# Gathering eight edges per index in the target stages of a three-layer graph network, with the layers' float32 split moved to ScalarE and TensorE

## The reference

```python
msg = h[src][:, None, :] * attn[src][:, :, None]
neigh = jax.ops.segment_sum(msg, dst, num_segments=n)
out = elu(neigh.reshape(n, -1) @ weight)
x = layernorm(x + out)
...
def layer(nf, traj, src, dst, We, be, Wn, bn):
    ef = concatenate([nf[src], nf[dst], traj[:, None]], -1)
    msg = leaky_relu(ef @ We.T + be, 0.01)
    red = segment_sum(msg, dst, nf.shape[0])
    return leaky_relu(concatenate([nf, red], -1) @ Wn.T + bn, 0.01)
# three layers, then layernorm(x + h)
```

## Time and profile before

| | us |
|---|---|
| median of 3 runs | 12386.24 (12385.78 to 12394.3) |
| span of the profiled execution | 10659.1 |
| grouping of the edges, attention scores | 2318 |
| source stage 0 / its target stage | 757 / 1382 |
| source stages 1, 2, 3 | 581, 579, 580 |
| target stages 1, 2, 3 | 1347, 1322, 1347 |

### The profile page before, as it was taken

One profiled execution on the slowest core, in us unless ns is written; L12 is line 12 of the kernel. 1 busy time (PEld: TensorE's weight loads), 2 busy tenths in 40 slices (PEclk: granted clock), 3 DMA queues, 4 the chain that ended last, 5 costly groups with the idle time before them and its releaser, 6 DMA issues. The chain is left out here.

```text
span 10659.1 us, 520405 instructions
## 1 busy us (share of the span) xinstructions
PE 8373.3 (79%) x180770; PEld 7503.4 (70%) x180770; DVE 9593.9 (90%) x19091; ACT 5558.6 (52%) x17135; POOL 5206.2 (49%) x5854
## 2 busy tenths in 40 slices
PE   7999999669976666589867776997777699766775
PEld 6999999347755555478766765886667678766774
DVE  6999999579989999778899996889999878899997
ACT  7888886027768888567422223673222267422222
POOL 0000000671027777534577773447777634577773
PEclk9999999569988888679988888998888799988887
DMA  1000000136556666758766675886766858766665
GB/s 43 9 8 8 8 8 7 38 93 216 216 185 195 195 195 195 132 184 294 247 193 200 204 204 89 291 294 210 205 205 205 167 173 295 255 194 202 205 204 89
DMA packets 1255800, 1748.08 MB, mean 164 GB/s; under 512 B 219360, under 2 KB 866418, under 8 KB 1254770
## 3 DMA queue, kind: packets, MB, share of 16 engines
q1 hardware_dynamic: 1009055, 1185.35, 34.1%
q0 software_dynamic: 245760, 549.71, 21.4%
q10 hardware_dynamic: 304, 4.93, 0.1%
HBM read 1049.39 MB, written 694.49 MB: 164 GB/s over the span
## 5 line engine op out<-in xcount | busy, mean ns | idle before, releaser
L1823 POOL DMA_INDIRECT work<-rows,quad_at x2928 | 2953.2, 1009 | 1028.6 <-issue 900.7
L1664 PE MATMUL bank<-work 128*128 128x64 bf16 x46848 | 2185.8, 209 | 997.8 <-DVE work L1911 997.5
L1664 PEld LDWEIGHTS bank<-work 128*128 128x128 fp8e4 (+1 forms) x46848 | 1979.2, 109 | 1062.6 <-issue 1033.2
L1848 ACT COPY work<-tabs 128x192 bf16 x2928 | 1029.4, 352 | 2942.2 <-PE bank L1864 2670.1
L1864 PE MATMUL bank<-work 128*128 128x64 bf16 x35136 | 1527.0, 208 | 274.2 <-DMA work<-hits_g 242.5
L1864 PEld LDWEIGHTS bank<-work 128*128 128x128 fp8e4 x35136 | 1382.8, 108 | 307.9 <-issue 235.6
L1608 PE MATMUL bank<-work 128*128 128x64 bf16 x34560 | 1565.2, 193 | 3.7 <-issue 3.7
L1608 PEld LDWEIGHTS bank<-work 128*128 128x128 fp8e4 x34560 | 1410.1, 98 | 175.3 <-issue 8.2
L1627 DVE TENSOR_SCALAR work<-bank,part 128x512 fp8e4<-128x512 f32 x1440 | 1026.8, 750 | 284.1 <-PE bank L1588 283.5
L1898 DVE TENSOR_TENSOR work<-bank,work 128x512 f32<-128x512 f32 x1464 | 1061.2, 739 | 238.3 <-PE bank L1864 138.2
L1695 POOL DMA_INDIRECT work<-rows,quad_at x976 | 990.1, 1014 | 416.3 <-PE bank L1664 216.8
(11 more groups left out here) (361 smaller groups left out, 18753.2 us busy)
## 6 DMA issues: line engine op xcount, KB each, us to landing
work<-hits_g SPq DMA_DIRECT2D x1464, 256.0 KB
rows<-work SPq DMA_DIRECT2D x1440, 256.0 KB, 3.3
hits_g<-work SPq DMA_DIRECT2D x976, 128.0 KB
rows<-work SPq DMA_DIRECT2D x480, 260.0 KB
work<-hits_s SPq DMA_DIRECT2D x720, 128.0 KB, 3.2
work<-rows,quad_at POOLq DMA_INDIRECT x3904
hits_s<-work SPq DMA_DIRECT2D x240, 128.0 KB
side<-meta POOLq DMA_DIRECT2D x720, 20.0 KB, 3.2
```

Source lines behind the costliest of these rows:

```text
L1664: last = ten.matmul(to[:, 0:D], hits_of(j), piece_of(j), start=j == 0 and k == 0, stop=j == QUAD - 1 and k == 2, skip_group_check=True)
L1823: pool.indirect_dma_start(quads[g // 2 % (GATHERED // 2)][:, half(g)], None, table, bass.IndirectOffsetOnAxis(ap=quad_at[:, g:g + 1], axis ...
L1848: sca.copy(window[q % 4].unsqueeze(1), tabs[:, 1, bass.ds(w, 1), :]).then_inc(s_window, 1)
```

## The change

An index names eight slots (an oct, two quads that lie together: 2 KB, 2,080 bytes in stage 0). So that the two quads lie together, the source stages store each group by itself: a partition writes two pieces of 1 KB. The number of groups of a target stage is 584 in place of 976, each with twice the slots; a group's stored matrices are 256 KB. The real groups (counted from `src` and `dst` of the reference by the kernel's numbering of slots) were 893 of the 976 and are 510 of the 584; the other 83 and 74 are the filling.

Stage 0 keeps its steps with operands twice as wide. In the layers everything goes by single groups: DVE adds (512 columns, PSUM and gathered rows, into `total`), and writes the leaky ReLU back to the PSUM bank of the group. ScalarE casts the bank to bf16 (`high`); TensorE subtracts that in the bank by a matmul with minus the identity (`minus_b`, 512 columns); ScalarE casts the rest (`mid`), TensorE subtracts again, ScalarE casts `low`. The scatter takes the three. POOL gathers four groups ahead of the add.

```diff
-NG = 976
+OCT = 8
+NG = 584
...
-        to_rows = table.rearrange("(l p g) c -> l p (g c)", p=P, g=GROUP_LOT)
+        to_rows = table.rearrange("(l g p) c -> l g p c", p=P, g=GROUP_LOT)
...
-                syn.dma_start(to_rows[bass.ds(l, 1), :, :].rearrange("l p c -> (l p) c"), made[n]).then_inc(s_out[n], 16)
+                syn.dma_start(to_rows[bass.ds(l, 1), :, :, :].rearrange("l g p c -> p (l g) c"),
+                              made[n].rearrange("p (g c) -> p g c", g=GROUP_LOT)).then_inc(s_out[n], 16)
...
-        HITS, AROUND, LAG, BATCH = 8, 16, 5, 4
+        AROUND, HITS, ROWS, WINDOWS, BANKS, MIDS, LOWS = 24, 8, 4, 4, 6, 6, 4
+        LESS, LESSER, SCATTER, KEEP = 2, 3, 5, 6
...
+                at_least(pool, s_added, g - ROWS + 1, since)
+                pool.indirect_dma_start(octs[g % ROWS], None, table_octs,
+                                        bass.IndirectOffsetOnAxis(ap=oct_at[:, g:g + 1], axis=0)).then_inc(s_octs[g % GATHERED], 16)
...
+                window_of(g, q)
+                if begun(g, LESSER + 3):
+                    low_of(g - LESSER - 3, (q - LESSER - 3) % AROUND)
+                if begun(g, LESS + 3):
+                    mid_of(g - LESS - 3, (q - LESS - 3) % AROUND)
+                if begun(g, 3):
+                    high_of(g - 3, (q - 3) % AROUND)
...
+                ten.matmul(z[q % BANKS][:, :], minus_b[:, :], high[q % BANKS], start=False, stop=True,
+                           skip_group_check=True).then_inc(s_less, 1)
...
+                vec.tensor_tensor(total[g % 2], z[g % BANKS][:, :], octs[g % ROWS], ALU.add).then_inc(s_added, 1)
...
+                vec.scalar_tensor_tensor(z[g % BANKS][:, :], total[g % 2], SLOPE, total[g % 2], ALU.mult, ALU.max).then_inc(s_leaky, 1)
```

More of the change, by code:

```diff
@@ L1660, in scatter_pieces @@
     def scatter_pieces(ten, to, hits_of, pieces):
[L1662 removed]
+        for j in range(OCT):
             for k, piece_of in enumerate(pieces):
[L1664 removed]
+                last = ten.matmul(to[:, 0:D], hits_of(j), piece_of(j), start=j == 0 and k == 0, stop=j == OCT - 1 and k == 2,
                                   skip_group_check=True)
@@ L1942, in target_phase @@
+            for g in range(NG + KEEP):
+                if g < NG:
+                    add(g)
+                if g >= KEEP:
+                    keep(g - KEEP)
+                if g < NG:
+                    leaky(g)
         block.__exit__(None, None, None)
```

277 lines of the change are left out of this document (136 added, 141 removed).

## The result

| | median, us | runs from - to |
|---|---|---|
| before | 12386.88 | 12385.78 - 12394.30 |
| after | 11172.48 | 11166.61 - 11181.81 |
| ratio | 0.9018 | 0.9005 - 0.9031 (95% interval) |

The kernel is faster by 1214 us. But the profile contradicts the sum at once: the profiled execution of after has a span of 11180.7 us and a time of 11181.81, so nothing lies around its span, while the span of before that I had read was 10659.1. By spans after is slower, by times it is faster.

The account below looks back on a forecast made before the run. POOL and DVE bind the layers' target-stage bodies, filling gathers the tails. Layers' target stages -533, stage 0 -114, source stages +12, renumbering -5: -640 from 12386, giving 11746 us; range 11,620 to 12,400.

Parts of the forecast that it names:

- I leave the 1727 us around it as they are: Whole kernel: the 1727 us between traced span and measured time stay constant, added to a forecast span of 10,019 us.
- nothing longer is added: Layers' target stages: beyond engine sums of 1.84 us and a 1.9 us ring, no longer term; 1.95 us per group taken.
- The lower bound of 11,620: Range's lower end for the kernel's time: 1.88 us per group in the layers, and the surroundings scaling with the span.
- TensorE's 1.84 us per group: Layers' target stages: 48 small matmuls at 0.029 us plus two of 512 columns at 0.22, at full clock.
- PE and ACT, both with 1.84: Layers' target stages: TensorE and ScalarE, each 1.84 us per group, replace POOL and DVE as what binds.
- the ring at 1.9: Layers' target stages: subtractions and casts between TensorE and ScalarE wait for each other, 1.9 us including two 0.2 us handovers.
- The rival of a low clock: Layers' bodies: waits lower TensorE's clock, 2.29 or 2.54 us per group, 12342 or 12780 us; chance within a shared 0.21.
- POOL 1.31 per gather, independent of the size: Layers' target stages: a gather costs POOL 1.31 us by its 128 indices; by bytes it would be 2.3.
- pays by bytes: Rival, filling groups at the target stages' tail: 3.77 us per gather, +133 us per layer, 12275 in all; chance 0.27.
- My choice, held for little better than even: Tail of the layers' target stages: a filling gather stays 1.884 us with twice the bytes, hidden under 1.95 per group.
- My lower bound: Stage 0's target stage: 2.08 us per group from VectorE's operations, below the chosen 2.16; upper bound 2.30.
- what will show it: Profile signs: layers' body 513 gathers per 1000 us, PE clock above 0.95, PE and ACT over 90% busy, DVE near 75%.

Follow-up runs that it names:

- laps of 12: After with the layers' target loop unrolled over 12 groups instead of 24, with 12 buffers of counts instead of 8: 9934.34 and 9938.59 us (kind A), 10702.81 (kind B).
- kind A: Conditions of a group of runs (chip or something else) where before takes about 10650 us; the trace read for the prediction is from it; after took 10832.42, ratio 1.0168.
- kind B: Conditions of a group of runs (chip or something else) where before takes about 12390 us; the result's times are from it; after took 11180.91 beside before, ratio 0.9023.
- the four buffers: After with 12 buffers of counts instead of 8, every lap still 24 groups: 11064.49 us on kind B, some 115 us gained by a single run.
- ScalarE relieved: Laps of 12 with the copy of a window moved from ScalarE to VectorE, three groups ahead of its add: 9929.33 us, stages of 1130 us.
- laps of 32: Before with the layers' target loop lengthened from 16 to 32 groups: 10758.47 us, 480 instruction packets, layers' target stages of 1338, 1418 and 1334 us.

## Why the prediction was wrong

The account by stages (us, from the first instruction of one stage to that of the next):

| stage | before A | after A | laps of 12, A | forecast | before B | after B | laps of 12, B |
|---|---|---|---|---|---|---|---|
| stage 0, source | 770 | 791 | 790 | +3 | 835 | 855 | 855 |
| stage 0, target | 1401 | 1241 | 1239 | 1268 | 1624 | 1242 | 1244 |
| layer, source (first) | 580 | 583 | 582 | +3 | 583 | 581 | 582 |
| layers, target | 1329, 1326, 1342 | 1456, 1437, 1430 | 1136, 1137, 1138 | 1161 | 1767, 1776, 1780 | 1522, 1492, 1476 | 1333, 1331, 1337 |

**The step that failed first is "I leave the 1727 us around it as they are".** Nothing lies around a span: every run's time is its span and 1.1 to 1.6 us. The trace of kind A and the times of kind B were two different bases. A difference of 16% that no row explains was a finding in itself, and I treated it as a constant. On kind B the target stages of before take 1549 us more than on kind A (223 in stage 0, 1326 in the layers), those of after 168 more (1 and 167). That difference makes the gain: stage 0 1624 to 1242, the layers 5323 to 4490, together 1215 less, which is the measured 1214 (the source stages and the rest differ by little), where on kind A the same four stages grow by 166. So the runs show where the gain arises, and not why kind B loses the time.

**The second is a missing term: TensorE's instructions.** The part on the layers' target stages costs matmuls, casts and handovers and says "nothing longer is added". It holds no word on the lap, which the change takes from 384 to 1200 matmuls. The term is 292 to 320 us per layer on kind A (1456 for 1136 and so on, the four buffers' share included), and with 300 the forecast's 1161 becomes 1461, for 1430 to 1456 measured. This term makes the kernel slower on kind A: stage 0 gives 160 us, the layers take 326, the first source stage 21, together 187 for the 180 of the medians. The "ISA Cache" section of the Trainium skill's page "Advanced Engine Details and Errata" has 128 KB for TensorE, and beside the diff's `AROUND` it would have made a rival.

The lower bound of 11,620 was not what it says: 1.88 us per group takes 123 us off 11,746, and the surroundings scaling another 104, which is 11,519. That too lies above 11,172.

**What held** on kind A, once laps of 12 take the second term away: the forecast for the span was 10,019 us and the measured one is 9935.5.
- *TensorE's 1.84 us per group*: 1.87 measured (800 us for 427 groups), granted clock 1.00. The 81 ns of the Trainium skill's page "TensorE: Matmul & The Clock Gate", section "Back-to-back issue gap", were no rival for the 48 small matmuls: they are for 128 columns, and these have 64. The trace of before contradicts them at 128 columns as well: in the grouping (L606) 6250 matmuls of 128 columns, each with its own weight load, start 57 ns (median) before the next one.
- *"PE and ACT, both with 1.84", the ring at 1.9*: half right. TensorE alone binds; ScalarE relieved by 105 us in 800 changes nothing. ScalarE's sum of 1.84 was right by luck: what follows a cast starts 0.48 us after it (5676.96 to 5677.44), not 0.53, and the window's copy holds ScalarE for 0.39 (5675.61 to 5676.00), not 0.25; 3 x 0.48 + 0.39 is 1.83. That the 0.2 us per handover cost nothing because two to three groups are between is argued, not shown by a run.
- *The clock*: 0.99 with laps of 12, as forecast from the source stages; 0.93 to 0.95 in after, where TensorE stops for the refetches (24 matmuls in 1.47 us behind a stop of 4.45). The rival of a low clock had the right side for kind A and the wrong cause.
- *POOL 1.31 per gather, independent of the size*: the mean was off, the reason isn't refuted. A gather of 2 KB pieces holds GpSimd for 1.26 to 1.27 us on average, for 1.01 with 1 KB, and stage 0's for 1.62 to 1.70 for 1.01. But the gathers that follow the one before at once (0.30 us) take a median of 0.97 us in laps of 12 (57 of 1752) and 0.96 in before (2840 of 2928, kind A). What makes the rest longer is open; it is hidden under 1.87 and 2.1 us. The page of after and, for before:

```profile
L1825 POOL DMA_INDIRECT work<-rows,oct_at x1752 | 2207.0, 1260 | 2277.1 <-DVE work L1948 2155.9
L1693 POOL DMA_INDIRECT work<-rows,oct_at x584 | 943.9, 1616 | 308.2 <-PE bank L1661 254.6
```

- *The tail*: the filling groups, laps of 12 on kind A:

```profile
6060.00:6180.00 120.00, 107.97 (x2763) 91.19 (x2762) 79.27 (x166) 102.08 (x222) 70.70 (x56) 1.00 1.01 245
```

56 gathers in 120 us, 2.14 us apart, for 1.884 in the earlier trace rows with half the bytes. So it costs at most (2.14 - 1.87) x 74 = 20 us a layer, not the 133 of the rival "pays by bytes". My choice, held for little better than even, came out right, a little too kind.
- *VectorE*: forecast 1.33 to 1.40 per group and near 75%; measured 837 of 1136 us, 1.43 (just above) and 74%.
- *Stage 0*: 2.16 per group, 1268; measured 1239 to 1244 on either kind, VectorE 1214 to 1216 of it, 2.08 per group. My lower bound was the value; the 0.08 on top (from the old period) had been something else.
- *Source stages*: +3 each, and the DMA share went to 0.91 or 0.92 for my 0.89 or 0.92. Right in the layers. Stage 0's source stage grew by 20 us on both kinds; on kind A the loss is spread evenly (1000 matmuls of TensorE take 47.5 us for 46), and its cause is open.

The signs in "what will show it" did their work: 383 gathers in 1000 us of body in place of 513, TensorE at 0.79 in place of over 0.9. The range failed because its base had two values. The missing lap term worked the other way: with laps of 12 the time on kind B is 10703, further below the range. No rival spoke of instructions.

## What to carry to other kernels

When a loop is unrolled over more groups, or a group gets more instructions, count the instructions of the busiest engine's lap, and look at the instruction queue's packets: they should not grow with the number of laps. With the lap shortened to 12 groups this version is faster than before on both kinds of chip (9934 to 9939 us, 0.932 to 0.933 of before, and 10703, 0.863). And where a trace's span and the timed runs disagree by per cents, the trace is of other conditions than the times; a change can gain on the one and lose on the other, as this one did (0.902 and 1.017).

## What the runs showed of the hardware

- The same program (before) took 10642 to 10694 us on six chips and 12382 to 12410 on two. Up to about 1950 us the executions agree within some 2 us; the source stages of the layers within 3 us (580 and 583).
- On kind B the time is lost where indirect DMAs of GpSimd run; TensorE's matmuls come in spurts 0.68 to 0.75 us apart in the layers, and 57% of the semaphore events of stage 0 are missing from the trace. Plain DMAs of GpSimd (480 in a source stage) bring neither.
- A refetched packet of 16 KB of TensorE's instructions has no single price: about 1.2 us in after on kind A (912 us for 778, the low clock behind it and the four buffers included), 0.7 in before with laps of 32 (92 us for 139), 0.5 on kind B (365 us for 779).
- An indirect gather on GpSimd took 1.01 us on average for 128 pieces of 1 KB, 1.26 for 2 KB, 1.6 to 1.7 for stage 0's of 2,080 bytes; back to back 0.96 and 0.97. A plain DMA of the same bytes took 0.54.
- Lanes that all read one address: 128 pieces of 1 KB took 1.884 us, 128 of 2 KB at most 2.14, so here nearly a cost per piece.
- Filling matmuls raised the granted clock of stage 0 from 0.52 to 0.98, and the stage went from 1623 to 1642 us.
